# Two-at-a-time becomes four-at-a-time: staggering the tiles of a retention layer and of the last layer, and a reordered vector queue in a cross-attention

## The reference

```python
# second cross-attention (L1_xattn): grouped queries, 16 heads of 16, 4 kv heads, 128 keys
s = (x@Wq) @ (ctx@Wk).T / 4 + alibi ; s = where(mask, s, NEG)
x = x + (softmax(s) @ (ctx@Wv)) @ Wo
# retention (L3_attn), two inner layers, 8 heads of 32, on h = layernorm(x)
r  = (q @ k.T * decay) @ v ; r = groupnorm(r) * gamma + beta
h1 = h + (silu(g) * r) @ Wo          # q, k, v, g = affine layernorm(h) @ W
h  = h1 + gelu(ln(h1)@W1 + b1)@W2 + b2
# last layer (L3_ffn): attention (16 heads of 16, causal, rope) and a mixture of 8 + 1 experts
h = n + attention(rmsnorm(n))        # n = layernorm(x)
out = h + shared(rms(h)) + sum_of_top2(w_e * expert_e(rms(h)))
```

## Time and profile before

| | |
|---|---|
| time, median of 3 runs | 4670.64 us (4670.5 to 4677.3) |
| the profiled execution | 4675.18 us, its span 4673.4 us |
| PE busy / DVE / ACT / POOL | 3670.6 / 2671.2 / 1728.8 / 364.9 us of the span |
| granted clock over the span | 0.775 |
| second cross-attention | 1160.8 to 1362.4 |
| retention layer | 3774.5 to 4264.2 |
| last layer | 4264.2 to 4666.8 |

### The profile page before, as it was taken

One profiled execution on the slowest core, in us unless ns is written; L12 is line 12 of the kernel. 1 busy time (PEld: TensorE's weight loads), 2 busy tenths in 40 slices (PEclk: granted clock), 3 DMA queues, 4 the chain that ended last, 5 costly groups with the idle time before them and its releaser, 6 DMA issues. The chain is left out here.

```text
span 4673.4 us, 70320 instructions
## 1 busy us (share of the span) xinstructions
PE 3670.6 (79%) x26668; PEld 2615.3 (56%) x26672; DVE 2671.2 (57%) x5440; ACT 1728.8 (37%) x3309; POOL 364.9 (8%) x566
## 2 busy tenths in 40 slices
PE   7999989978668788637887769788888866676777
PEld 5555558867545565514555435355555545555666
DVE  6898884432557877864444542467676533334444
ACT  4888871112343443412222122344444312221222
POOL 3000000000000000001010001111121101110000
PEclk7555559988876666667887889899999967777677
DMA  2000001000010000000000140000000020000000
GB/s 73 1 0 0 0 22 46 0 18 2 12 45 1 0 0 0 27 28 7 4 4 5 55 127 0 3 5 2 2 2 4 0 110 0 0 0 0 0 0 9
DMA packets 43768, 72.12 MB, mean 15 GB/s; under 512 B 25693, under 2 KB 33377, under 8 KB 40293
## 3 DMA queue, kind: packets, MB, share of 16 engines
q1 hardware_dynamic: 35432, 70.54, 4.3%
q10 hardware_dynamic: 8256, 0.52, 0.2%
HBM read 67.91 MB, written 3.15 MB: 15 GB/s over the span
## 5 line engine op out<-in xcount | busy, mean ns | idle before, releaser
L1315 DVE TENSOR_SCALAR_CACHE_REDUCE l0x_ex<-l0x_s_ps 128x1024 f32<-128x1024 f32 x258 | 305.6, 1222 | 57.1 <-PE l0x_s_ps L1018 56.1
L1150 ACT ACTIVATE l0x_ex<-l0x_ex,l0x_neg_max,l0x_q_scale 128x2048 f32<-128x2048 f32 x128 | 268.0, 2094 | 51.7 <-DVE l0x_neg_max L1321 49.9
L1018 PE MATMUL l0x_s_ps<-l0x_kT,l0x_qT 64*128 64x512 bf16 x516 | 230.2, 587 | 35.3 <-ACT l0x_qT L1145 19.7
L1030 PEld LDWEIGHTS l0x_t_ps<-l0x_identb,l0x_pb 128*128 128x128 bf16 x2048 | 195.7, 140 | 109.8 <-issue 51.6
L1157 ACT ACTIVATE l0x_pt<-l0x_t_ps 128x1024 bf16<-128x1024 bf16 x256 | 246.1, 1013 | 25.9 <-PE l0x_t_ps L1030 25.8
L1030 PE MATMUL l0x_t_ps<-l0x_identb,l0x_pb 128*128 128x128 bf16 x2048 | 229.6, 300 | 9.2 <-ACT l0x_pt L1157 4.1
L1330 DVE TENSOR_SCALAR l0x_pb<-l0x_ex 128x2048 bf16<-128x2048 f32 x128 | 156.3, 1222 | 0.0
L262 PE MATMUL l3x_bank<-l3x_wproj,l3x_cat 128*128 128x256 f32 x512 | 121.9, 393 | 33.2 <-DVE l3x_cat L3340 33.2
L262 PE MATMUL l3x_bank<-l3x_w_kv_x,l3x_ctxT 128*128 128x512 f32 x256 | 130.2, 657 | 0.9 <-ACT l3x_ctx_q L761 0.9
L262 PEld LDWEIGHTS l3x_bank<-l3x_wproj,l3x_cat 128*128 128x128 f32 x512 | 96.9, 194 | 53.7 <-DVE l3x_cat L3340 39.8
L1018 PEld LDWEIGHTS l0x_s_ps<-l0x_kT,l0x_qT 64*128 64x128 bf16 x516 | 48.8, 119 | 130.2 <-issue 76.2
(11 more groups left out here) (738 smaller groups left out, 8811.8 us busy)
## 6 DMA issues: line engine op xcount, KB each, us to landing
l3x_wproj<-in_L_xattn_wproj SPq DMA_DIRECT2D x1, 4096.0 KB, 22.4
l3a_w<-in_L_attn_W SPq DMA_DIRECT2D x2, 2048.0 KB, 12.8
l2f_w<-in_L_ffn_w SPq DMA_DIRECT2D x1, 2816.0 KB, 11.4
l0x_ctxT<-in_ctxT SPq DMA_DIRECT2D x8, 256.0 KB, 2.9
l0a_wq<-in_L_attn_W_Q SPq DMA_DIRECT2D x1, 2048.0 KB
l0a_wk<-in_L_attn_W_K SPq DMA_DIRECT2D x1, 2048.0 KB
l0a_wv<-in_L_attn_W_V SPq DMA_DIRECT2D x1, 2048.0 KB, 7.8
l0a_wo<-in_L_attn_W_O SPq DMA_DIRECT2D x1, 2048.0 KB, 13.1
```

Of the source, the lines that this page charges most:

```text
L1018: ins = mm(s_ps[:, j * 512:(j + 1) * 512], qT[rows, h // 2, :], kT[rows, h // 2, j * 512:(j + 1) * 512], start=True, stop=True)
L1030: ins = nc.tensor.transpose(t_ps[:, j * P:(j + 1) * P], pb[:, h % 2, j * P:(j + 1) * P], identb[:])
L1150: s.activation(ex[:, h % 4, :], ex[:, h % 4, :], ACT.Exp, scale=q_scale[:, h:h + 1], bias=nb[:, h:h + 1], accum_out=sums[:, h:h + 1]).then ...
L1315: v.tensor_scalar(ex[:, h % 4, c], s_ps[:, c], 1.0, None, ALU.mult, ALU.max, accum_out=mx[:, h, half:half + 1]).then_inc(o.up(scores_taken ...
```

## The change

*Second cross-attention:* on DVE, `add_bias` and the layer norm of tile t+2 move from behind `shift(ahead, 1)` to between `take_q` and `shift(ahead, 0)`, and the bias is now that of tile t+1. The extra zero row of `neg` and one bias ahead of the loop go. On PE, the transposes of `mix` become a function `turn`, and `turn(t, 0)` comes ahead of the wait for `k_ready`.

*Retention layer:* four tiles at a time in two banks each, written out without a loop; way n starts `n * 5 // 2` segments later (0, 2, 5, 7), a tile is 20 segments long, and a way goes on to its second tile without waiting for the others. The five norms of a tile become two, `hid` shares the memory of `scores`, the product for g moves from the q/k/v segment to the mix segment, three more `yield`s split long segments, and PE also waits for `v_ready` ahead of the scores.

*Last layer:* the same with a stagger of 8 segments and 32 segments per tile. The attention is written out anew: ACT writes the exponentials straight into the block diagonal of `pb`, v gets a column of ones, and DVE divides the mixed output (128x256) in place of the probabilities. The experts work one deep in one bank. The clearing of four `pb` comes ahead of the first norm on DVE. In the diff the lines removed from this layer's TensorE program (calls of `Attention.tensor` and `Moe.tensor`) are left out; what replaces them is shown whole.

```diff
+    def __init__(self, L, name, eps, centred=True, primed=False, uses=1, turns=True):
...
+        self.have_var, self.have_rstd, self.normed = (L.sig(f"{name}_{n}", uses) for n in ("have_var", "have_rstd", "normed"))
+        if turns:
+            self.yT = L.sb(f"{name}_yT", [P, DC, P])
+            self.turned, self.ready = L.sig(f"{name}_turned", uses, primed), L.sig(f"{name}_ready", uses)
+
+    def vector(self, o, x, k=None):
...
-            def mix(t, g):
+            def turn(t, g):
                 for n in (2 * g, 2 * g + 1):
                     pe.wait_ge(exped.sem, exped.value(t, n + 1))
                     for h in range(4):
                         ins = nc.tensor.transpose(t_bank[n % 2][:, h * P:(h + 1) * P], e[:, 4 * n + h, :], env.ident[:])
                     ins.then_inc(pT_ps.sem, 1)
+
+            def mix(t, g):
...
                     heads(t + 1, True)
+                pe.wait_ge(tile_done.sem, tile_done.value(t, 0))
+                turn(t, 0)
+                if more:
                     pe.wait_ge(k_ready.sem, k_ready.value(t + 1))
-                pe.wait_ge(tile_done.sem, tile_done.value(t, 0))
                 mix(t, 0)
                 if more:
                     score(t + 1, 0)
                     values(t + 1)
+                turn(t, 1)
                 mix(t, 1)
                 if more:
...
                 if more:
                     take_q(ahead)
+                    add_bias(o, t + 1)
+                    ahead.t = t + 2
+                    whole(norm.vector(ahead, tile_of(env.x, t + 2)))
+                    ahead.t = t + 1
                     shift(ahead, 0)
...
                 if more:
                     shift(ahead, 1)
-                    add_bias(o, t + 2)
-                    ahead.t = t + 2
-                    whole(norm.vector(ahead, tile_of(env.x, t + 2)))
                 dve.wait_ge(y_ps.sem, y_ps.value(t))
...
-            v.memset(neg[:, TILES:TILES + 1, :], 0.0).then_inc(first.up(), 1)
...
             add_bias(first, 0)
             shift(first, 0)
             shift(first, 1)
-            add_bias(first, 1)
             whole(norm.vector(second, tile_of(env.x, 1)))
...
-    LAYERS_, H, HD, FF = 2, 8, 32, 1024
+    LAYERS_, H, HD, FF, WAYS = 2, 8, 32, 1024, 4
...
+            ret, cur, hid = L.sb("ret", [P, D]), L.sb("cur", [P, D]), sc
+            norm, inner = Norm(L, "ln", 1e-5), Norm(L, "inner", 1e-5, uses=2 * LAYERS_)
+            dve_bank, act_bank = bank
...
-                    xT = n1[l].yT
-                    yield from n1[l].tensor(pe, t, bank[3])
-                    pe.wait_ge(n1[l].ready.sem, n1[l].ready.value(t))
+                    xT = inner.yT
+                    yield from inner.tensor(pe, t, act_bank, 2 * l + 1)
                     yield
-                    for n, ps in (("q", bank[0]), ("k", bank[1])):
+                    pe.wait_ge(inner.ready.sem, inner.ready.value(t, 2 * l + 1))
+                    for n, ps in (("q", dve_bank), ("k", act_bank)):
...
-                    project(nc, bank[3][:, 0:D], lambda c: xT[:, c, :], lambda c: w["g"][:, l, c, :], DC).then_inc(vg_ps.sem, 1)
+                            project(nc, ps[:, m * P:(m + 1) * P], lambda c: w[n][:, l, c, m * P:(m + 1) * P], lambda c: xT[:, c, :], DC)
+                    project(nc, act_bank[:, D:2 * D], lambda c: xT[:, c, :], lambda c: w["v"][:, l, c, :], DC).then_inc(qkv_ps.sem, 1)
                     yield
...
+                    pe.wait_ge(v_ready.sem, v_ready.value(t, k))
...
                     pe.wait_ge(scores_ready.sem, scores_ready.value(t, k))
-                    pe.wait_ge(v_ready.sem, v_ready.value(t, k))
+                    project(nc, act_bank[:, 0:D], lambda c: xT[:, c, :], lambda c: w["g"][:, l, c, :], DC).then_inc(g_ps.sem, 1)
                     for h in range(H):
...
                     ins.then_inc(ygT_ps.sem, 1)
+                    yield
                     pe.wait_ge(ygT_ready.sem, ygT_ready.value(t, k))
-                    project(nc, bank[2][:, 0:D], lambda c: ygT[:, c, :], lambda c: w["o"][:, l, c, :], DC).then_inc(ret_ps.sem, 1)
...
+                    project(nc, dve_bank[:, 0:D], lambda c: ygT[:, c, :], lambda c: w["o"][:, l, c, :], DC).then_inc(ret_ps.sem, 1)
+                    yield from inner.tensor(pe, t, act_bank, 2 * l + 2)
+                    yield
+                    pe.wait_ge(inner.ready.sem, inner.ready.value(t, 2 * l + 2))
...
                     pe.wait_ge(hid_ready.sem, hid_ready.value(t, k))
...
+                yield
...
-        tiles = [one_of_two(n, bank[4 * n:4 * n + 4]) for n in range(2)]
...
         block = L.block()
+
+        def in_its_turn(n, program, eng):
+            yield from steps(n * 5 // 2)
+            for t in range(TILES // WAYS):
+                yield from program(eng, t)
 
...
             L.tag = str(n)
             order = L.orders()
+            first, other = bank
...
+
+                def turn(n):
+                    for i in range(4):
+                        ins = nc.tensor.transpose(bank[n % 2][:, i * P:(i + 1) * P], pb[:, 4 * n + i, :], env.ident[:])
+                    ins.then_inc(pT_ps.sem, 1)
+
+                def add_expert(i):
+                    return mm(first[:, 0:D], hidT[:], w_out[:, i, 0, :], start=i == 0, stop=i == NE - 1)
+
+                yield
+                yield from rms.tensor(pe, t, other, 1)
+                yield
+                pe.wait_ge(rms.ready.sem, rms.ready.value(t, 1))
+                project(nc, first[:, 0:P], lambda c: down[:, c, :], lambda c: rms.yT[:, c, :], DC).then_inc(heads_ps.sem, 1)
+                yield
+                pe.wait_ge(lat_v_ready.sem, lat_v_ready.value(t, 1))
                 for m in range(DC):
+                    r, r2 = slice(m * P, (m + 1) * P), slice(D + m * P, D + (m + 1) * P)
+                    mm(first[:, r], qa_lat[:, r], lat[:], start=True, stop=True)
+                    mm(first[:, r2], qb_lat[:, r], lat[:], start=True, stop=True)
+                    mm(other[:, r], ka_lat[:, r], lat[:], start=True, stop=False)
+                    project(nc, other[:, r], lambda c: ka_x[:, c, r], lambda c: rms.yT[:, c, :], DC, start=False)
+                    ins = project(nc, other[:, r2], lambda c: kb_x[:, c, r], lambda c: rms.yT[:, c, :], DC)
+                ins.then_inc(heads_ps.sem, 1)
+                yield
+                pe.wait_ge(qk_ready.sem, qk_ready.value(t, 1))
+                mm(first[:, 0:D], lat[:], v_lat[:], start=True, stop=True).then_inc(heads_ps.sem, 1)
                 yield
                 pe.wait_ge(qk_ready.sem, qk_ready.value(t))
+                pe.wait_ge(lat_v_ready.sem, lat_v_ready.value(t, 2))
+                for i in range(H):
+                    for b in range(2):
+                        r = slice(b * S, (b + 1) * S)
+                        ins = mm(bank[i // 8][r, (i % 8) * S:(i % 8 + 1) * S], qT[:, i, r], kf[:, i // 8, r], start=True, stop=True)
+                ins.then_inc(scores_ps.sem, 1)
+                yield from steps(2)
+                pe.wait_ge(exped.sem, exped.value(t))
+                for n in (0, 1):
+                    turn(n)
+                yield
+                for n in (2, 3):
+                    pe.wait_ge(pT_ready.sem, pT_ready.value(t, n - 1))
+                    turn(n)
+                yield
+                for n in (3, 4):
+                    pe.wait_ge(pT_ready.sem, pT_ready.value(t, n))
+                for i in range(H):
+                    ins = mm(first[:, i * HV:(i + 1) * HV], pt[:, i, :], vv[:, i, :], start=True, stop=True)
+                ins.then_inc(out_ps.sem, 1)
+                yield
+                pe.wait_ge(out_ready.sem, out_ready.value(t))
+                for c in range(DC):
+                    ins = nc.tensor.transpose(other[:, c * P:(c + 1) * P], out[:, 8 * c:8 * c + 8, :].rearrange("p h d -> p (h d)"), env.ident[:])
+                ins.then_inc(out_ps.sem, 1)
+                yield
+                pe.wait_ge(outT_ready.sem, outT_ready.value(t))
+                project(nc, first[:, 0:D], lambda c: outT[:, c, :], lambda c: wo[:, c, :], DC).then_inc(out_ps.sem, 1)
+                yield from rms.tensor(pe, t, other, 2)
+                yield
+                pe.wait_ge(rms.ready.sem, rms.ready.value(t, 2))
+                mm(first[:, 0:8], env.ones_row[:, 0:P], router_b[:], start=True, stop=False)
+                project(nc, first[:, 0:8], lambda c: rms.yT[:, c, :], lambda c: router_w[:, c, :], DC, start=False).then_inc(logits_ps.sem, 1)
+                for i in range(NE):
+                    yield
+                    if i:
+                        pe.wait_ge(hidT_ready.sem, hidT_ready.value(t, i))
+                    project(nc, other[:, 0:2 * I], lambda c: rms.yT[:, c, :], lambda c: w_in[:, c, i * 2 * I:(i + 1) * 2 * I], DC).then_inc(hid_ps.sem, 1)
+                    if i:
+                        add_expert(i - 1)
+                    yield
```

(88 more changed lines are left out.)

256 lines of the change are left out of this document (124 added, 132 removed).

## The result

The changed kernel takes 4535.67 us (4520.55 to 4539.74, four runs) against 4673.64 for the kernel before: a ratio of 0.9699, 95% interval 0.9674 to 0.9723. The forecast was 4500, the range 4430 to 4595. The time is in the range, and 36 us above the number named.

The account below looks back on a forecast made before the run. No engine was taken to bound the layers throughout: PE's waits in queue-ordered chains and a clock below its higher level were winnable. Savings 41 + 87 + 43 = 171 from 4675.2 give 4504, less 4.5: 4500 us, range 4430 to 4595.

Parts of the forecast that it names:

- case A: Whole kernel, the outcome as forecast: 4465 to 4560 us, the upper end keeping the whole loss to the clock; chance 0.50.
- The new order of VectorE: Cross-attention: bias and norm moved, q waits only for ACT (23.7), first bias gone (2.3), last residual add earlier (4.8).
- the transposes: Cross-attention: PE's transposes run beside the copy of k, saving 0.78 us in each of 7 tiles, 5.5.
- The clock gave back 29 of the 46 us: Retention layer: 46 us of PE's 341.6 busy were the lower clock level's cost; half was taken as won.
- the 335 counted for the higher clock: Last layer: length over 88 turns at the higher level, five full cycles of 37 us plus filling, emptying and clearing.
- the 79 us of lower level: Last layer: PE's busy 288.5 against 209 at the higher level; half taken as won, a third of that hidden.
- 2 for small waits: Last layer: allowance of 2 us in each tile's eight-turn cycle, 35 plus 2 giving 37.
- B: Both four-way layers and cross-attention: PE fed steadily, higher clock throughout, 229 us saved, 4442; chance 0.16.
- C: In-order queues cost twice the count: retention's waits grow by 45, last layer's tile takes 50, 4588 us; chance 0.24.
- D: Retention and last layers: the clock falls as small matmuls lie between dense ones, near 4850 us; chance 0.05.
- E: Retention and last layers: no overlap is won, only the cross-attention's 36 to 41 us stay, 4634; chance 0.05.
- F: ACT: every table switch holds it 1.4 us longer, 22 us in the last layer, 4522; chance 0.03, counted in case A.

Follow-up runs that it names:

- the last layer in step: Changed kernel plus eight semaphore increments, last layer's four tiles started together (stagger 0, not 8), retention ways one segment apart: 4499.54 us, ratio 0.9628; last layer 324.5.

## Why the prediction held, and where not

The time fell where case A had it (4465 to 4560).

**Cross-attention, right** (41 forecast, 42.5 measured). The new order of VectorE was put at 23.7 + 2.3 + 4.8 = 31 with its share of the clock on top, and brought 34.0; the transposes 5.5, and brought 8.5. The period of 18 to 19 and q released by ACT came as said; VectorE's wait for scores fell from 5.82 to at most 1.1.

**Retention layer, right in number** (400.0 against 403). At the higher level 380 was counted: 295 of PE's work and 85 of waits. Measured: 312.3 busy and 87.8 idle. The 20 turns that repeat take 187.2 us (two score groups of the same way, 3812.67 and 3999.89), 181 counted. The clock gave back 29 of the 46 us, half was assumed; that half was a choice between two bounds and not worked out, so a miss of only 3 us is in part luck. The waits are where I put them, on the normed tile and on `y`, but up to 4.0 long in place of under 3. Table loads: 26, about 27 counted. The premise behind it, that stages must be staggered to overlap, was wrong; it didn't hurt the sum, which was counted turn by turn.

**Last layer, right mechanism, term mis-sized** (30.0 against 43). The layer is 37.7 us above the 335 counted for the higher clock, where 25 were allowed. The five full cycles, put at 37, took 41.8 (scores at 4241.67 and, five tiles on, 4450.83), 24 us more, and the rest lies in filling, emptying and clearing. Two terms were too small. The clock: I took half of the 79 us of lower level as won, and PE's busy time is 271.8, still 63 above the 209: 17 were won. And a wait is missing from the chain: the second norm behind the next tile's rotation and spreading, 3.3 to 5.4 us a cycle, in the place of which I had "2 for small waits":

```profile
4235.57 2.36 DVE L4186 TENSOR_TENSOR l3f_qT<-l3f_qf,l3f_own 128x1024 f32<-128x1024 f32 x2
...
4238.11 0.34 DVE L224 TENSOR_SCALAR l3f_rms_y<-l3f_h,l3f_rms_rstd 128x256 f32<-128x256 f32 x1
4238.51 0.69 PE L241 MATMUL l3f_bank<-ident,l3f_rms_y 128*128 128x128 f32 x2 [4.32 <-DVE l3f_rms_y L224]
```

The profile was to show the exponentials as PE's longest wait; they hold 18.1 us, the normed tile 53.2. Clearing the four buffers put the first statistics at 10.8 us, 9 counted.

**What the sum left out**: that untouched layers stay as they are. Four instructions fewer on VectorE cost 19.6 us, some 1,600 us further on and in none of my cases. With 9 us too much for the three layers (171 against 162) this makes 29 of the 36 us between 4500 and 4535.67; the other 7 are within the scatter of other layers between executions.

**The rivals.** B (the higher clock throughout) didn't come: 0.86, 0.87 and 0.79. C is true in part: VectorE's in-order queue cost the last layer more than I counted, 41.8 a tile, but not 50, and the retention layer's waits were as counted. D is refuted by PE's busy time, which fell in both layers, and E by both layers' lengths. F: a load takes 1.28 us and the next exponential starts 1.30 behind its start (4291.34 and 4292.64 in the last layer). The Trainium skill (ScalarE: Activation LUTs, What ACT_TABLE_LOAD costs) adds a drain of about 1.38 us to each switch of tables; this trace shows none, as the earlier trace rows showed none.

## What to carry to other kernels

When more tiles are put in flight on in-order queues, try the phase between them as a parameter of its own, zero included: here it was worth 80 us of 355 in one layer and 48 of 325 in the other, and the number of turns did not rank the phases. Count ScalarE's table loads in each phase too. When an edit changes how many instructions an engine has, look at every long hardware loop behind it on that engine (here one of 270 instructions), for waits without a releaser and for packets on the instruction queues; a few idle increments ahead of it may be worth more than the edit. Compare layer by layer, the untouched ones too.

## What the runs showed of the hardware

A loop of 270 VectorE instructions either costs nothing to fetch or five packets of 8 KB and a wait of 1.9 to 2.2 us in each round behind the first, by a shift of four instructions. All fourteen profiles agree with the loop's place in their kernel's program.

TensorE's clock doesn't follow how busy it is alone. In the last layer in step, mixing with v (128x17 products) and what follows kept PE busy 20.00 of 20 us at 0.50. Behind it come a wait of 4.0 us, the norm's transposes and the router, and then the experts, which ran at 0.99:

```profile
4170.00:4190.00 20.00, 20.00 (x91) 19.64 (x92) 2.05 (x6) 1.53 (x4) 0.00 (x0) 0.50 0.00 1
4190.00:4210.00 20.00, 15.97 (x58) 13.30 (x57) 14.03 (x61) 6.31 (x17) 3.19 (x8) 0.67 0.00 0
4210.00:4230.00 20.00, 19.92 (x93) 16.25 (x93) 6.08 (x20) 7.01 (x29) 0.00 (x0) 0.99 0.00 1
```

That is the window of the earlier trace rows again, with four tiles in place of two. The version with the least idle time there has the lowest clock of the four (0.77), so it seems that the 50 us that PE's work is still above the 209 counted for the higher level are not to be had by closing gaps alone. No run shows that, nor what would give them.
